# Gated recurrence: first fill ahead of the output step, output matrices in two buffers, query projection behind the second level's first fill

## The reference

```python
q, k, v = (xn @ Wq.T), (xn @ Wk.T), (xn @ Wv.T)       # 16 heads of 64
alpha, aR = sigmoid(xn @ Wa.T + ba), sigmoid(xn @ WaR.T + baR)
beta, gamma = sigmoid(xn @ Wb.T + bb), sigmoid(xn @ Wg.T + bg)
def step(carry, inp):
    S, R = carry
    kn = k_t / max(norm(k_t), 1e-12)
    pred = einsum('bhji,bhj->bhi', S, kn)
    r = clip(v_t - pred, -1, 1)
    S = a_t[..., None] * S
    S = S + b_t * kn[..., None] * (v_t - kn @ S)[..., None, :]
    o = einsum('bhji,bhj->bhi', S, q_t)
    R = aR_t[..., None] * R
    R = R + g_t * kn[..., None] * (r - kn @ R)[..., None, :]
    return (S, R), o + einsum('bhji,bhj->bhi', R, q_t)
out = os @ Wo.T + residual
```

## Time and profile before

| | us |
|---|---|
| median of 3 runs | 2977.55 |
| lowest and highest run | 2961.21, 2988.56 |
| the profiled execution | 2989.19 |
| its span, first to last instruction | 2987.4 |
| mean granted TensorE clock over the span | 0.896 of 2.4 GHz |

### The profile page before, as it was taken

One profiled execution on the slowest core, in us unless ns is written; L12 is line 12 of the kernel. 1 busy time (PEld: TensorE's weight loads), 2 busy tenths in 40 slices (PEclk: granted clock), 3 DMA queues, 4 the chain that ended last, 5 costly groups with the idle time before them and its releaser, 6 DMA issues. The chain is left out here.

```text
span 2987.4 us, 115613 instructions
## 1 busy us (share of the span) xinstructions
PE 2398.5 (80%) x49947; PEld 1861.7 (62%) x49947; DVE 1954.5 (65%) x4625; ACT 1363.1 (46%) x3250; POOL 1002.2 (34%) x1250
## 2 busy tenths in 40 slices
PE   8987478999976578888778887669998997797754
PEld 6754465555555577777777776548776654575633
DVE  3448335777756787888777888157777666564752
ACT  5443133444443344454444542447776553563420
POOL 0000324556650345434543355311111440360004
PEclk9979677999997799999999999969999998897876
DMA  3200331111110000000000000012221003242014
GB/s 99 66 1 29 114 116 53 47 47 46 47 58 3 3 4 4 4 4 4 4 4 4 4 4 4 3 27 61 63 62 58 4 3 108 64 110 66 5 43 122
DMA packets 80270, 117.47 MB, mean 39 GB/s; under 512 B 11490, under 2 KB 66034, under 8 KB 79234
## 3 DMA queue, kind: packets, MB, share of 16 engines
q1 hardware_dynamic: 71250, 100.31, 10.9%
q0 software_dynamic: 8576, 10.53, 1.7%
HBM read 98.16 MB, written 16.51 MB: 38 GB/s over the span
## 5 line engine op out<-in xcount | busy, mean ns | idle before, releaser
L2469 POOL TENSOR_SCALAR l1xs_p<-l1xs_p,l1xs_col 128x257 f32<-128x257 f32 x256 | 234.3, 936 | 204.4 <-DVE l1xs_col L2425 204.4
L3173 PE MATMUL psum<-l1d_rw,l1d_cols 64*32 64x48 f32 x16384 | 188.1, 211 | 106.1 <-issue 76.1
L3173 PEld LDWEIGHTS psum<-l1d_rw,l1d_cols 64*32 64x32 f32 x16384 | 164.4, 108 | 128.5 <-issue 118.1
L2390 ACT ACTIVATE l1xs_p<-psum,l1xs_col 128x257 f32<-128x257 f32 x256 | 119.7, 473 | 209.6 <-DVE l1xs_col L2420 203.5
L3429 DVE TENSOR_TENSOR l1d_rw<-l1d_rw,l1d_tots 128x1536 f32<-128x1536 f32 (+1 forms) x96 | 141.4, 1473 | 64.9 <-PE psum L3173 64.3
L2945 POOL TENSOR_TENSOR l1d_kc<-l1d_ms,l1d_beta 128x512 f32<-128x512 f32 x16 | 17.5, 1093 | 494.9 <-DVE l1d_ms L3484 477.9
L2432 DVE STREAM_TRANSPOSE l1xs_pt<-l1xs_p 128x288 f32<-128x288 f32 x256 | 122.4, 478 | 79.1 <-POOL l1xs_p L2469 79.0
L3112 PE MATMUL psum<-XN,l1d_wp 128*128 128x128 f32 x1024 | 142.6, 296 | 7.6 <-issue 6.7
L3112 PEld LDWEIGHTS psum<-XN,l1d_wp 128*128 128x128 f32 x1024 | 130.6, 206 | 21.0 <-issue 17.8
L2354 PE MATMUL psum<-l1xs_pt,l1xs_vals 32*128 32x512 f32 x1152 | 136.6, 604 | 0.0
L2342 PE MATMUL psum<-l1xs_keys,l1xs_qx 128*32 128x257 f32 x2048 | 132.7, 392 | 3.7 <-DVE l1xs_qx L2414 1.9
(11 more groups left out here) (563 smaller groups left out, 6852.7 us busy)
## 6 DMA issues: line engine op xcount, KB each, us to landing
l2f_w<-in_l2f_w SPq DMA_DIRECT2D x16, 768.0 KB
l1xs_vals<-in_ctx_strips SPq DMA_DIRECT2D x16, 576.0 KB
l0f_w<-in_l0f_w SPq DMA_DIRECT2D x15, 579.0 KB
l0x_ctxT<-in_ctxT SPq DMA_DIRECT2D x16, 516.0 KB, 3.7
l1xs_keys<-in_ctxT SPq DMA_DIRECT2D x16, 516.0 KB
l2x_ctxK<-in_ctxT SPq DMA_DIRECT2D x64, 129.0 KB, 2.1
l2x_ctxV<-in_ctxT SPq DMA_DIRECT2D x64, 129.0 KB, 2.1
l3f_w<-in_l3f_w SPq DMA_DIRECT2D x15, 193.5 KB
```

What stands on the lines that cost most here:

```text
L2390: nc.scalar.activation(p[:, t % 4, :S2], score_ps(t)[:, :S2], ACT.Exp, bias=col[:, 0, t % 4:t % 4 + 1], accum_out=col[:, 1, t % 4:t % 4 + ...
L2469: nc.gpsimd.tensor_scalar(p[:, t % 4, :S2], p[:, t % 4, :S2], col[:, 2, t % 4:t % 4 + 1], None, ALU.mult).then_inc(s["norm"], 1)
L3173: mm = nc.tensor.matmul(k.ps[bank0 + pr + e // per * 2][b * T:b * T + T, e % per * w:(e % per + 1) * w], columns[rr, at:at + T], moving[rr ...
```

## The change

The diff does five things in `l1_attn`. The output matrices of odd tiles go to a second buffer, `wideN`, laid over a buffer that the layer norm no longer needs and zeroed by GpSimd; so `widen` of matrices 1 and 2 waits for the output step of the tile before the last one, not of the last one. On TensorE the first fill of the next tile stands ahead of the output step; the output projection moves from the round's end to behind the next round's values; the query projection moves from behind the values to behind S level 1. On ScalarE the output copy moves behind the widening, the columns and `widen_x`. On VectorE `result` moves behind `advance_s` of level 0.

```diff
--- before.py
+++ after.py
@@ -2840,6 +2840,8 @@
         ll = sb("ll", [128, 2, 2, H, T // 2])
         wideM, wideX = sb("wideM", [128, 5, H, 64]), sb("wideX", [128, 2 * H, 64])
         v, u, rd, ya = (sb(n, [128, 1024]) for n in ("v", "u", "rd", "ya"))
+        wideN = norm.bufs[5][:].rearrange("p c j d -> p (c j d)").rearrange("p (n h t) -> p n h t", n=2, h=H)
+        output = lambda i, j: wideM[:, j] if i % 2 == 0 else wideN[:, j - 1]
         kc, lt, xi = sb("kc", [128, T * T]), sb("lt", [128, T * (T + 1)]), sb("xi", [128, T * (T + 1)])
         tmp, wmat = sb("tmp", [128, 1024]), sb("wmat", [128, 128])
         block = ph.enter_context(nc.Block())
@@ -2873,6 +2875,8 @@
             nc.gpsimd.memset(wideM[:], 0.0).then_inc(s["zero"], 1)
             pool.wait_ge(s["zero"], 2)
             nc.gpsimd.memset(xi[:, 0:T * T:T + 1], 1.0).then_inc(s["zero"], 1)
+            pool.wait_ge(norm.s["cols"], NCH)
+            nc.gpsimd.memset(wideN, 0.0).then_inc(s["zero"], 1)
             tt = nc.gpsimd.tensor_tensor
 
             def blocks(x, m):
@@ -3026,11 +3030,13 @@
                 x, f = ((ms, 1), (ms, 2), (mr, 0), (ll, 0), (ll, 1))[j]
                 needs = ("p_mm", "o_mm", "o_mm", "z_mm", "z2_mm")[j]
                 act.wait_ge(s["scaled"], i + 1)
-                if i > 0:
-                    act.wait_ge(s[needs], i * 2)
+                ahead = 1 if j in (1, 2) else 0
+                if i > ahead:
+                    act.wait_ge(s[needs], (i - ahead) * 2)
+                to = output(i, j) if ahead else wideM[:, j]
                 x = x[:, i % 2, f] if j >= 3 else x[:, i % 2, :, f, :]
                 for h in range(2):
-                    y = wideM[:, j, :, 32 * h + (16 if j >= 3 else 0):32 * h + 32]
+                    y = to[:, :, 32 * h + (16 if j >= 3 else 0):32 * h + 32]
                     sign = 2 if j in (0, 3, 4) else 0
                     ins = activation(y, x, ACT.Identity, scale=part[:, sign + h:sign + h + 1])
                 ins.then_inc(s["wideM"], 1)
@@ -3060,7 +3066,7 @@
             take_gate(0, 1)
             take_gate(0, 0)
             columns(0)
-            act.wait_ge(s["zero"], 3)
+            act.wait_ge(s["zero"], 4)
             for i in range(NT + 2):
                 old, mid, new = 0 <= i - 2 < NT, 0 <= i - 1 < NT, i + 1 < NT
                 if old and i <= NT:
@@ -3087,15 +3093,14 @@
                 if mid:
                     widen(i - 1, 3)
                     widen(i - 1, 0)
-                if old:
-                    take(i - 2, "o_mm", rd, "B", "o")
-                if mid:
                     widen(i - 1, 1)
                     widen(i - 1, 2)
                 if new:
                     columns(i + 1)
                 if mid:
                     widen_x(i - 1, 0)
+                if old:
+                    take(i - 2, "o_mm", rd, "B", "o")
                 if i == NT:
                     take(i - 1, "v_mm", v, "A", "v")
 
@@ -3275,8 +3280,8 @@
                     for r in range(2):
                         rr = slice(64 * r, 64 * r + 64)
                         out = k.ps[bank("B") + r][64 * (h % 2):64 * (h % 2) + 64, h // 2 * 64:h // 2 * 64 + 64]
-                        nc.tensor.matmul(out, u[rr, h * 64:(h + 1) * 64], wideM[rr, 1, slot(h), :], start=True, stop=False)
-                        mm = nc.tensor.matmul(out, ya[rr, h * 64:(h + 1) * 64], wideM[rr, 2, slot(h), :], start=False,
+                        nc.tensor.matmul(out, u[rr, h * 64:(h + 1) * 64], output(i, 1)[rr, slot(h), :], start=True, stop=False)
+                        mm = nc.tensor.matmul(out, ya[rr, h * 64:(h + 1) * 64], output(i, 2)[rr, slot(h), :], start=False,
                                               stop=True)
                         if h == H - 1:
                             mm.then_inc(s["o_mm"], 1)
@@ -3306,12 +3311,14 @@
                 now, old, mid, new = i < NT, 0 <= i - 2 < NT, 0 <= i - 1 < NT, i + 1 < NT
                 if old and i <= NT:
                     values(i - 2)
-                if new:
-                    project_q(i + 1)
+                if 3 <= i <= NT:
+                    step_out(i - 3)
                 if old and i != NT + 1:
                     step_y(i - 2)
                 if now:
                     fill_s(i, 1)
+                if new:
+                    project_q(i + 1)
                 if new:
                     project_k(i + 1)
                 if old:
@@ -3348,12 +3355,12 @@
                     broadcast(i + 1)
                 if now:
                     fill_r(i, 4)
-                if old:
-                    step_o(i - 2)
                 if new:
                     fill_0(i + 1, 0)
                     fill_0(i + 1, 1)
                 if old:
+                    step_o(i - 2)
+                if i >= NT:
                     step_out(i - 2)
                 if i == NT:
                     values(NT - 1)
@@ -3558,11 +3565,12 @@
                     turn(i - 1)
                 if now:
                     keep_s(i, 0)
+                if now:
+                    keep_r(i, 0)
+                    advance_s(i, 0)
                 if i >= 3:
                     result(i - 3)
                 if now:
-                    keep_r(i, 0)
-                    advance_s(i, 0)
                     advance_r(i, 0)
                     advance_s(i, 1)
                     keep_s(i, 1)
```

## The result

The change makes the kernel slower. Measured side by side on one chip, the kernel after takes 3035.12 us (median of four runs, 3023.64 to 3041.7), the kernel before 2974.13 us: a ratio of 1.020, 95% interval 1.0142 to 1.0258. That is +61 us, where +22 was forecast. The profiled execution took 3037.72 us (span 3035.8) against 2989.19, +48.5 us.

The account below looks back on a forecast made before the run. TensorE and VectorE hand work to each other, neither full, with TensorE also paced by instruction supply. Thirteen rounds +15.6, first rounds +4.4 and end +1.8 give +22 us on 2977.55: about 2999 us, range 2960 to 3027.

Parts of the forecast that it names:

- The step that failed: Query projection behind S level 1, which ends at S: +1.5 us a round, bounds 0 and +2.0.
- S + 8.8 less S + 7.3: Start of step u, counted from S, the end of S level 1: S + 8.8 after the change, S + 7.3 before.
- The fill order: First fill ahead of the output step on TensorE: -0.3 us a round, bounds -1.0 and +0.3.
- Rival 2, the clock,: TensorE's waits at the first fill drop it to 1.2 GHz, each second round losing 1.7 us: about 3012 us; chance 0.13.
- Rival 1, that the supply takes it in,: Instruction stalls absorb the query projection's 2.0 us: 2963 or 2946 us; chance 0.16 within 1%, 0.13 for a larger gain.
- its own test: Rival 1 holds if a round's stalls behind S level 1 shrink by as much as the moved query projection takes.
- The first rounds: First two rounds, without output step: the query projection leaves a free wait and follows the fill; +4.4 us, bounds +1 and +6.
- The end: Last rounds: ScalarE widens before copying tile 14's output, +3.5; one round earlier about -1.7; together +1.8 us, bounds -2 and +4.

Follow-up runs that it names:

- the repair in the kernel before: Kernel before with the query projection behind S level 1; ScalarE copies y and widens X and corner ahead of the query copies: 1.0041, against 1.0129 without that ScalarE order.
- the one in the changed kernel: Kernel after with ScalarE's copies of y ahead of the query copies: 1.0122 of before; with widening of X and corner ahead too: 1.0139.
- 3 long products: Kernel after with 3 unused products of 128x512 on TensorE in the wait ahead of each first fill: 1.0153 of before.
- the second profile of the same kernel: Kernel after, unchanged, run once more beside later experiments: 1.0186 of before, 64.28 us a round.
- The two kernels with the query projection put back: Kernel after with the query projection ahead of S level 1: 1.0072 of before; the second also with y, X and corner ahead of ScalarE's query copies: 1.0115.
- the kernel with all repairs: Kernel after with query projection ahead of S level 1, y, X, corner first on ScalarE, 3 unused 128x512 products, early output copy in last rounds: 1.0074 of before.
- thirteen short ones: Kernel after with 13 unused products of 128x64 on TensorE ahead of each first fill: 1.0189 of before.

## Why the prediction was wrong

The sign of the sum was right and its size a third: +22 against +61. The profiled execution came out 26.7 us above its forecast: 15.1 of it is the query projection in the twelve rounds, 8.8 the fill order there, whose sign was wrong, 11.3 the end, and 1.5 a later start of the stage; the last piece of the rounds (-3.1), the first rounds (-1.9) and the rest of the kernel (-5) lie on the other side.

**The step that failed** is this one, of the query projection: "its copies at about S + 2.7, those of y (two, near 0.6 us each like the key's) at S + 3.7, X at S + 6.0", and from it the price of 1.5 us. It lists ScalarE's queue rightly, and then asks only who needs the *last* of it, step u. The copies of y have a nearer customer, the key projection directly behind the query projection on TensorE:

```python
            def project_k(i):
                if i > 0:
                    pe.wait_ge(s["kn"], i * 2)
                if i >= 3:
                    pe.wait_ge(s["y"], i * 2 - 4)
                projected(i, 1, bank("A"), "k_mm")
```

By the prediction's own numbers, the copies of y end at S + 3.7 and TensorE is free for the key projection at S + 1.95: a wait of 1.8 us. It stood there to be read off, and it measures 1.81. The term came to +2.76 us a round (3.49 - 0.73) instead of +1.5, outside its bound of +2.0, and the repair in the kernel before puts the wait at 0.9%, the one in the changed kernel at 0.5 to 0.8%. Step u then starts 9.3 us after S level 1 in the mean (24.18 and 14.85 us after the first fill's start), so late that its key copies were never waited for: the wait that the prediction looked for there was overtaken by the one it missed. So u came 2.6 us later after S level 1, where the prediction had S + 8.8 less S + 7.3. Half of that miss is in the value before: S + 7.3 is from one round, in which a stall of 1.91 us lay, and the mean of the twelve is S + 6.76.

**The bare place of the query projection** was +1.0 us a round where the wait is removed, against +1.5 with bounds 0 and 2.0. That stalls give some of it back was right in part: those in the two pieces behind S level 1 fell by 0.5 us a round, and the total of the twelve rounds did not fall. The Trainium skill ("Runtime: NRT & Kernel Launch", instruction fetch mechanics) calls the crossing of an instruction block mostly hidden. The traces disagree again, if "issue" is that supply as the prediction worked out: 46.5 us of it before the fills in twelve rounds of the kernel after.

**The fill order** is the second step that failed: -0.3 with bounds -1.0 and +0.3, it measured +0.43 in one profile of the kernel after and +0.9 in the other (+0.8 in the two with y copied first). The first rows were ready when the prediction said (a wait of 3.58). But the sum took 1.14 us for each half and they took 1.75, at 1.2 GHz, which also left 0.71 of the second wait where 1.4 was foretold: the fill ends 7.8 us after R level 4 (3.59 + 4.21) and not 7.1, where it ended before (7.72), so that the 0.7 us by which VectorE was to start sooner are gone. With 3 long products ahead of it, it ends at 7.46. The forecast that S level 1 starts 16.3 us after R level 4 stands against 16.7 and 17.2 measured and 16.6 before.

**Rival 2, the clock,** was right in kind: the stretch at 1.2 GHz stood at each first fill, where the prediction priced it in every second round. "None shows it for 3.4 us alone" was the honest state of the evidence. Now seven of thirteen stretches begin within a wait of about 3.6 us or at its end; the other six were under way before it. The Trainium skill ("TensorE: Matmul & The Clock Gate", on the clock gate) has an idle TensorE drop to 1.2 GHz, and the trace agrees, with 0.50 for 6.8 us around that wait. I gave it 0.13, which the page and the row at 6.9 us should have raised. Its worth was small all the same, about 0.3% as far as the 3 long products show it.

**Rival 1, that the supply takes it in,** is refuted as a whole. Stalls before fills fell from 63.5 to 46.5 us (about 50 foretold) in one profile and to 56.7 in the other. By its own test, the stalls between S level 1 and the next R level 4 would have shrunk by 2.0 us a round: they went from 7.3 to 6.3 us in the first profile and to 7.4 in the second. What did shrink, from 2.0 to 0.4 us in both, are those ahead of S level 1, where TensorE now waits for the rows instead.

**The first rounds** came to +3.7 us for three, against 5.6 foretold.

**The end** was forecast at +1.8 and was +13.1. TensorE's timeline has the last two output projections, before:

```profile
1873.00 2.05 PE L3292 MATMUL psum<-l1d_rd,l1d_wo 128*128 128x128 f32 x16 [1.06 <-ACT l1d_rd L2977]
1911.69 2.05 PE L3292 MATMUL psum<-l1d_rd,l1d_wo 128*128 128x128 f32 x16 [1.78 <-ACT l1d_rd L2977]
```

and with the change:

```profile
1915.64 3.79 PE L3297 MATMUL psum<-l1d_rd,l1d_wo 128*128 128x128 f32 x16 [3.88 <-ACT l1d_rd L2981]
1963.57 3.79 PE L3297 MATMUL psum<-l1d_rd,l1d_wo 128*128 128x128 f32 x16 [5.21 <-ACT l1d_rd L2981]
```

The copy of the output behind the widening did what was said in the last round: the output projection waited 5.21 us for it where it had waited 1.78, so +3.4 for the +3.5 foretold. One round earlier y no longer waited the 1.86 us for the v copies, as foretold, but the projection waited 3.88 us instead of 1.06, which is more. Most of the rest is the clock. From y of tile 14 to y of tile 15, in the two kernels:

```profile
1878.60:1917.30 38.70, 22.15 (x596) 19.88 (x597) 8.72 (x13) 16.20 (x26) 22.57 (x39) 0.91 0.01 2
```

```profile
1919.30:1970.70 51.40, 32.64 (x597) 29.47 (x596) 9.42 (x13) 16.26 (x26) 22.53 (x39) 0.65 0.01 1
```

The same matmuls, 596 and 597, kept TensorE busy for 22.15 and 32.64 us; on this path nothing covers them. In the second profile of the same kernel this stretch took 44.3 us (1928.42 to 1972.72) and the end 134.0, so some 7 us of the 13 come and go between executions, and by that profile the change costs 5.5 there. The kernel before has one profile, so how far its own end varies is not known.

**What the fill order costs, and what stays open.** The two kernels with the query projection put back are slower than before by 0.7 and 1.15%. The trace of the second, which has no wait for the copies of y, says where. Its four pieces are 20.38, 4.02, 7.59 and 30.05 us: the first is 2.37 us longer than before, the others together 0.76 shorter. That is 19 us in twelve rounds; its first three rounds are 5 us shorter (164.9) and its end is 14 us longer (142.2), 28 us in all or 0.9%. Its largest wait for VectorE, with those of the earlier trace rows to compare:

```profile
PE psum L3178 <- DVE l1d_rw L3404: 55.5, 25, 3.7
```

The 2.37 us are half idle time and half clock. In the first piece TensorE idles 4.7 us where it idled 3.5 (the waits for the rows are new; most of the stalls and the wait for `l1d_tots` are gone in return), and the two halves of the fill take 3.5 us without their wait where they took 2.3. So the wait that the output step used to cover now stands open, the output step follows it, and TensorE's list, not VectorE's, sets the start of S level 1. In the kernel with all repairs, which has the 3 long products, the first piece is 19.83 us, so these returned 0.55 of the 1.2 us of the clock. Open is which of the moves that stand beside the fill order costs what: the kernel with the old list of VectorE and the new one of TensorE was not run. In the traces of single executions the rounds also differ by less than the medians do (1.26 us a round between the kernel after with y, X and corner first and the kernel before with the late projection and the same repair, 15 us of 29), and some 7 us of each end may be of its execution alone.

## What to carry to other kernels

Before a step is moved on one engine, write down for each engine that copies its result what stands behind that copy in its list, and for each of those who waits for it first: an in-order queue hands the delay to everyone behind, and the nearest customer sets the price, not the last. A step that covers a wait can be worth up to its whole length (here 1.0 of 2.0 us for the query projection); taken out of the wait to "start the next thing sooner" it goes onto the path elsewhere, and the thing starts no sooner if its input isn't ready. Where a move opens an idle gap of some 3.6 us on TensorE, price the work behind it at 1.2 GHz. And take the value before from the mean of the rounds, not from one round with a long stall in it.

## What was unexpected in the hardware

With a wait of about 3.6 us ahead of each first fill and one of 0.7 in it, the granted clock was 0.50 at every one of them, for 6.8 or 13.6 us at twelve of thirteen. Six of these stretches began before the wait, in or behind idle times of 0.7 to 3.0 us. Three products of 128x512 in that wait brought the mean back to 0.95 and thirteen short ones to 0.94, but neither ended such stretches, and the short ones brought no gain. At the end of the stage the mean clock was 0.65 in one execution, and another execution of the same kernel was 7 us faster in that stretch. And time at 1.2 GHz was cheap where it fell into waits: 3 long products took it from about 167 to 76 us (2 x 0.05 x 758) in the twelve rounds, and the median fell by 8 us.
